# Stores moved to ScalarE's queue, evictions ahead of the first exponential, and a new order of loads and of image 0 in a linear attention layer

## What is computed

```
g = x as (image, h, w, 32 groups, 8); gn = (g - mean) / sqrt(var + 1e-5)      # over h, w and the 8
q, k, v = split(gn @ W_qkv)                                                     # 256 channels each
k = softmax(k over the 4096 tokens)
context = k^T v                                                                 # 256 x 256 for each image
out = x + ((q @ context) @ W_out + b_out)
```

## Time and profile before

| | us |
|---|---|
| median of 3 runs | 1199.64 |
| lowest, highest | 1195.49, 1200.19 |
| profiled execution, its time | 1202.58 |
| its span | 1200.6 |
| TensorE busy in the span | 1166.4 (97%) |
| ScalarE, VectorE, GpSimd busy | 836.3, 931.0, 627.0 |

### The profile page before, as it was taken

How to read it: one execution, slowest core, us unless ns; L and a number is a source line. 1 busy time by engine, 2 the same in 40 slices (tenths; PEclk the granted TensorE clock), 3 DMA queues, 4 the chain that set the end, 5 groups by cost and what they waited for, 6 DMA issues and landing times.

```text
span 1200.6 us, 21468 instructions
## 1 busy us (share of the span) xinstructions
PE 1166.4 (97%) x8206; PEld 1089.3 (91%) x8206; DVE 931.0 (78%) x2008; ACT 836.3 (70%) x1146; POOL 627.0 (52%) x305
## 2 busy tenths in 40 slices
PE   4999999999999999999999999999999999999998
PEld 3889999989899898998989999899999989999996
DVE  6988779787796877878787797878869788796561
ACT  5667768677685776857777676776857768577764
POOL 7655563645656355553655636456463655536530
PEclk9999999999999999999999999999999999999999
DMA  8438666586766758657486665867657586573524
GB/s 318 163 134 315 228 216 236 179 296 214 258 212 202 263 188 280 228 201 250 165 316 228 215 232 179 303 212 261 214 199 271 179 295 227 198 254 119 190 84 162
DMA packets 107078, 266.70 MB, mean 222 GB/s; under 512 B 10208, under 2 KB 10208, under 8 KB 106976
## 3 DMA queue, kind: packets, MB, share of 16 engines
q1 hardware_dynamic: 106976, 265.33, 63.7%
HBM read 198.18 MB, written 67.11 MB: 221 GB/s over the span
## 4 chain that ended last, share of the span: by engine, by line
PE 82%; DMA 6%; DVE 4%; ACT 3%; issue 2%; POOL 1%; SPq 1%; DVEq 0%; ACTq 0%; POOLq 0%
PE ps_k L460 24%; PE ps_e L625 18%; PE ps_e L634 9%; PE ps_e L542 5%; PE ps_e L554 5%; PE ps_e L544 5%; DMA xs<-in_xt_dram 4%; PE ps_g L554 4%; PE ps_g L544 4%; PE ps_g L542 4%; PE ps_g L573 1%; PE ps_g L590 1%; DMA x_raw<-in_xn_dram 1%; DVE bn L922 1%; DVE e_raw L1054 1%
## 5 line engine op out<-in xcount | busy, mean ns | idle before, releaser
L387 POOL TENSOR_TENSOR xt_lo<-xt_raw,xt_hi 128x1024 fp32r<-128x1024 f32 x128 | 307.5, 2404 | 458.8 <-ACT xt_hi L738 194.1
L393 POOL TENSOR_TENSOR x_lo<-x_raw,x_hi 128x1024 fp32r<-128x1024 f32 x128 | 282.4, 2225 | 59.9 <-ACT x_hi L743 50.5
L994 DVE TENSOR_TENSOR mx<-ps_k,mx 128x256 f32<-128x256 f32 x480 | 203.1, 423 | 72.0 <-ACT e_raw L747 50.2
L795 ACT ACTIVATE o_stage<-ps_e,bias 128x512 f32<-128x512 f32 x253 | 168.8, 687 | 105.5 <-PE ps_e L634 101.5
L460 PE MATMUL ps_k<-wk_hi,xt_hi 128*128 128x256 f32 x1024 | 205.9, 283 | 1.4 <-DVE mx L994 1.2
L460 PE MATMUL ps_k<-wk_lo,xt_hi 128*128 128x256 f32 x1024 | 205.0, 282 | 0.0
L747 ACT ACTIVATE e_raw<-ps_k 128x512 f32<-128x512 f32 x256 | 141.2, 595 | 78.1 <-PE ps_k L460 78.1
L755 ACT ACTIVATE e_hi<-e_raw 128x1024 fp32r<-128x1024 f32 x128 | 134.8, 1053 | 67.2 <-DVE e_raw L1054 45.4
L922 DVE BATCH_NORM_STATS2 bn<-xs 128x6 f32<-128x512 f32 x240 | 153.8, 685 | 33.2 <-DMA xs<-in_xt_dram 31.9
L460 PEld LDWEIGHTS ps_k<-wk_hi,xt_hi 128*128 128x128 f32 x1024 | 164.3, 189 | 10.6 <-issue 2.4
L460 PE MATMUL ps_k<-wk_hi,xt_lo 128*128 128x256 f32 x1024 | 157.5, 282 | 0.0
(11 more groups left out here) (147 smaller groups left out, 2027.6 us busy)
## 6 DMA issues: line engine op xcount, KB each, us to landing
xt_raw<-in_xt_dram SPq DMA_DIRECT2D x128, 512.0 KB, 4.6
x_raw<-in_xn_dram SPq DMA_DIRECT2D x128, 512.0 KB, 3.8
out_dram<-o_stage SPq DMA_DIRECT2D x127, 512.0 KB, 4.5
xs<-in_xt_dram SPq DMA_DIRECT2D x240, 256.0 KB, 5.0
w_setup<-in_w_dram SPq DMA_DIRECT2D x2, 256.0 KB, 9.7
out_dram<-o_stage SPq DMA_DIRECT2D x2, 256.0 KB, 2.0
wk<-in_w_dram SPq DMA_DIRECT2D x1, 256.0 KB, 10.0
wq_t<-in_w_dram SPq DMA_DIRECT2D x1, 256.0 KB, 11.0
```

The source lines that it names most:

```text
L387: nc.gpsimd.tensor_tensor(xt_lo[:, s], xt_raw[:, s], xt_hi[:, s].bitcast(F32), ALU.subtract).then_inc(xt_lo_ready, 1)
L393: nc.gpsimd.tensor_tensor(x_lo[:, s], x_raw[:, s], x_hi[:, s, :, 0:C].bitcast(F32), ALU.subtract).then_inc(x_lo_ready, 1)
L795: nc.scalar.activation(o_stage[:, u % O_SLOTS, h, :], src, ACT.Identity, bias=bias[:, h:h + 1]).then_inc(o_ready, 1)
L994: nc.vector.tensor_tensor(mx[:], tile, mx[:], ALU.max).then_inc(max_done, 1)
```

## The change

**ScalarE and the stores.** Each store is taken from SyncE's program and stands in ScalarE's, behind the second eviction of its chunk; ScalarE first waits for `o_ready`, that is, for its own eviction to have written. The last chunk is stored in two halves there. ScalarE's DMAs go on a queue of their own.

**ScalarE's order in a period.** The eviction of emit 4 is put ahead of `exps(n, 0)`. `xt_high(n, 2)` is put behind the gathers' exponentials and `wk_high`.

**SyncE's order.** It has no stores any more. The halves of `xs` go behind other emits (`XS_AHEAD` for `XS_AFTER`), and the last `xt` chunk of a period is loaded in the next one, behind its second `x` load.

**VectorE's order in a period.** The statistics halves are spread otherwise: ten stand ahead of `key_maxes(n, 3)` where eight stood, and one stands between the block maximum and `shift(n, 0)` where four stood.

**Image 0.** Loads of `x` go two steps later, behind `xs` halves 6 to 9; VectorE has two more statistics halves ahead of the first maximum, and none left between the second block maximum and the shifts there; TensorE's gather takes `gather_high(0, 2)` ahead of `gather_low(0, 1)` and `gather_high(0, 3)` ahead of `gather_low(0, 2)`, and the two statistics products later; GpSimd has one `e_low` fewer and `xt_low` of the next image later; ScalarE has the exponentials ahead of the `xt` work.

```diff
-XS_AFTER = {0: (4, 8), 2: (8, 12), 3: (12, 16)}
-FIRST_XT = (8, 11, 15)
-POOL_LOW = 3
+XS_AHEAD = {0: (4, 8), 1: (8, 12), 2: (12, 14), 4: (14, 16)}
+FIRST_XT = (11, 13, 15)
+FIRST_X = (6, 7, 8, 9)
+POOL_LOW = 2
...
             for q in range(S_SLOTS, CB * NCH):
-                if q < 2 * X_SLOTS:
-                    load_x(0, q - X_SLOTS)
                 sp.wait_ge(bn_done, NCH * CB + q - S_SLOTS + 1)
                 load_xs(1, q)
+                if q in FIRST_X:
+                    load_x(0, FIRST_X.index(q))
...
                 for j in range(X_SLOTS, NCH):
                     sp.wait_ge(g_ps, b * NCH + (j - X_SLOTS + 1))
                     load_x(b, j)
+                    if more and b and j == X_SLOTS + 1:
+                        sp.wait_ge(e_ps, b * (CB * NCH))
+                        load_xt(n, 1 - parity, EMIT_ORDER[NCH - 1])
...
-                    if b == B - 1 and u == NCH - 1:
-                        store_last()
-                    elif not late(b, u, CB - 1):
-                        store(b, u)
-                    if more2 and u in XS_AFTER:
-                        for q in range(*XS_AFTER[u]):
+                    if more2 and u in XS_AHEAD:
+                        for q in range(*XS_AHEAD[u]):
                             sp.wait_ge(bn_done, b * (NCH * CB) + 2 * NCH * CB + q - S_SLOTS + 1)
                             load_xs(b + 2, q)
...
+                def first_gather():
+                    gather(0, 0)
+                    gather_high(0, 1)
+                    gather_high(0, 2)
+                    gather_low(0, 1)
+                    spread_max(0, 1)
+                    gather_high(0, 3)
+                    gather_low(0, 2)
+                    gather_low(0, 3)
+                    gather(0, 4)
+                    stats_mean(1)
+                    gather(0, 5)
+                    gather_high(0, 6)
+                    stats_var(1)
+                    gather_low(0, 6)
+                    gather(0, 7)
...
+            def store(b, u):
+                act.wait_ge(o_ready, b * (CB * NCH) + CB * u + CB)
+                nc.scalar.dma_start(out_chunks[bass.ds(b * NCH + EMIT_ORDER[u], 1)].rearrange("a p h n -> (a p) h n"),
+                                    o_stage[:, u % O_SLOTS]).then_inc(stored[u % O_SLOTS], 16)
...
             def emit(b, u):
                 for h in range(CB):
                     if not late(b, u, h):
                         emit_half(b, u, h)
+                        if b == B - 1 and u == NCH - 1:
+                            store_half(b, u, h)
+                        elif h == CB - 1:
+                            store(b, u)
...
+                if b == 0:
+                    exps(0, 3)
+                    x_high(0, 4)
+                    xt_high(1, 1, 0)
+                    scales(0)
+                    for j in range(HALF, NCH):
+                        exp_high(0, j)
+                        if j < NCH - 1:
+                            x_high(0, j + 1)
+                        exp_exact(0, j)
+                    xt_high(1, 1, 1)
...
                 both_out(4)
+                emit(b, 4)
                 if more:
                     exps(n, 0)
-                emit(b, 4)
...
-            for q in range(1, 5):
+            for q in range(1, 7):
                 bn_half(1, q)
             for j in range(HALF):
                 key_maxes(0, j)
-                for q in ((5, 6), (7, 8), (9,), ())[j]:
+                for q in ((7, 8), (9, 10), (11,), ())[j]:
                     bn_half(1, q)
...
                 key_maxes(n, 2)
-                bn_halves(4, 8)
+                bn_halves(4, 10)
                 key_maxes(n, 3)
                 block_max(n, 0)
                 block_diag(n, 0)
-                bn_halves(8, 12)
+                bn_halves(10, 11)
                 shift(n, 0)
```

More of the change, by code:

```diff
@@ L329, in period @@
                     load_x(b, j)
-                if not more:
-                    for u in range(LATE[0][0], NCH):
-                        store(b - 1, u)
+                    if more and b and j == X_SLOTS + 1:
+                        sp.wait_ge(e_ps, b * (CB * NCH))
+                        load_xt(n, 1 - parity, EMIT_ORDER[NCH - 1])
                 if more2:
@@ L341, in period @@
                 for u, j in enumerate(EMIT_ORDER):
-                    if more2 or (more and j not in DOUBLED):
+                    if u < NCH - 1 and (more2 or (more and j not in DOUBLED)):
                         sp.wait_ge(e_ps, b * (CB * NCH) + CB * u + CB)
@@ L680, in period, with gather_steps @@
                 n, np_ = b + 1, 1 - parity
[L681 to L698 removed]
+                def first_gather():
[14 more added lines that the diff above has]
+                    gather(0, 7)
+                def gather_steps():
+                    gather_high(b, 0)
+                    if more:
+                        stats_mean(n)
+                    gather_low(b, 0)
+                    gather_high(b, 1)
+                    spread_max(b, 1)
+                    if more:
+                        stats_var(n)
+                    gather_low(b, 1)
+                    for j in range(2, NCH):
+                        gather(b, j)
+                if b == 0:
+                    first_gather()
+                else:
+                    gather_steps()
                 if more:
@@ L861, in period @@
                     emit_half(b - 1, *LATE[0])
+                    store(b - 1, LATE[0][0])
                 u_high(b, parity)
@@ L865, in period @@
                     emit_half(b - 1, *LATE[2])
+                    store(b - 1, LATE[2][0])
                 else:
@@ L1164, in _ @@
             key_maxes(0, 4)
-            bn_half(1, 11)
+            bn_half(1, 13)
             key_maxes(0, 5)
```

109 lines of the change are left out of this document (49 added, 60 removed).

## The result

The changed kernel takes 1240.15 us in the median of 4 runs (1234.63 to 1244.68) against 1197.82 of the kernel before (4 runs): ratio 1.0353, 95% interval 1.0316 to 1.0391. It is 42 us slower; the prediction was 7 us faster. The profiled execution took 1234.63 us, with a span of 1232.5.

A forecast was written before the change was run, and what follows sets the result against it. TensorE was taken as the bound, with only its idle time and lower clock to win back. Steady images -5.5, image 0 -4.0 + 1.5, stores +1.0 gave -7.0: 1199.64 to 1192.6 us, 8-in-10 range 1188.5 to 1199.5.

The forecast's parts named there:

- Steady images: the eviction wait: Images 2 to 14: TensorE's wait for emit 4's eviction, 4.9 us over the span, is removed in full where it occurs.
- h: ScalarE's hold by one store: about 0.5 us, with up to 1.56 us possible before TensorE waits.
- That count: From emit 4's end to emit 6's first half: TensorE needs 8.54 us, ScalarE 6.98 us plus the store's hold.
- The term of 1.0 us: Stores on ScalarE in the steady images: 1.0 us allowed in all for new small waits of TensorE.
- Rival 4: Stores on a second queue share the engines, so `x` or `xs` loads land later: 1197.6 us, chance 0.05.
- Rival 5: Store issues on ScalarE wait for SyncE's, delaying emit 6 by 1.04 us in 14 images: 1207.2 us, chance 0.08.
- `x_lo` wait: Late gathers: TensorE's wait for GpSimd's low part of `x`, 2.5 us in 5 waits, goes or nearly.
- Rival 1: Steady images: the median run holds only half of the 5.5 us of waits, giving 1195.4 us; chance 0.17.
- Rival 3: Steady images: the stall only moves by one emit, leaving image 0's gain alone: 1198.1 us, chance 0.08.
- The keys: Image 0: two more statistics halves ahead of the first maximum cost 1.5 us, bounds 0 and 2.5.
- The gather's waits: Image 0: five TensorE waits of 3.59 us; with 1.7 us of missing clock, 4.0 us taken back.
- rival 2: Image 0 gives nothing, as VectorE's delay in the keys cancels the gather's gain: 1195.1 us, chance 0.10.

The follow-up runs named there:

- b_stats_new: The kernel before with only the changed kernel's order of the steady statistics halves, all stores on SyncE's queue: 1291.08 us, ratio 1.0767.
- a_both_undone: The changed kernel with the stores back on SyncE and the steady statistics halves in their old places: 1198.63 us, ratio 0.9998.
- b_steady_rest: The kernel before with the changed kernel's steady-image edits except the stores and VectorE's statistics order: 1197.58 us, ratio 0.9994.

## Why the prediction was wrong

**The term that was missing: the statistics ahead of the maxima.** The step that failed is the one under "Steady images: the eviction wait". It counted: "three of the four statistics halves between block maximum and shift are gone", and never charged the place to which two of them went. VectorE does them ahead of `key_maxes(n, 3)`, with `spread_max` behind it, for which TensorE waits. By the prediction's own data a first price was at hand: two halves of 0.65 us and a wait of 1.70 for `xs`, 3.0 us an image, 42 in 14 images. Measured: `u_hi` comes 3.0 us later (28.1 for 25.1), and since TensorE came for it only at 25.9, its step begins 2.2 us later, some 31 us in 14 images; the edit costs 30.5. That the first price gives the same 3.0 is luck: what sets the time is the landing of half 9 at 23.1 us, and in b_stats_new the same two halves make `u_hi` 5.9 us late. For image 0 the prediction did this very sum and put a price on it; for the 14 images that count it did not.

**The size of the slack: the stores on ScalarE.** h was forecast at 0.5 us and measured 0.57. The issue was forecast at 0.39 us and measured 0.38. The failing step is "At 0.5 nothing shows on TensorE by the count above; ... I allow 1.0 us". That count, 8.54 against 6.98 us, ran from emit to emit alone. ScalarE also evicts the keys of the next image in between, and the last of these start a chain (maxima, block diagonal, variance parts) with TensorE at its end. Its slack ended below 0.54 us, not at 1.56. The term of 1.0 us measured 14, of which the hold alone is 5; the rest is mostly the collision of emit 2's store with the `xs` loads, for which the sum had no term.

**Rival 4 was right in kind.** It had a load that lands later since a store shares the engines, priced at the wait for `x_lo` that doubles. It was `xs`, and 5 to 7.6 us. That the rival too stood 5 us above the sum is luck, since its price was that of another load. As the Trainium skill has it ("DMA: Bandwidth & Descriptors", Issuing engines are not separate DMA queues), DMAs of two issuers interleave on the same engines: the landings of the table agree, a store that went from 24.5 to 26.3 us beside loads that went from 25.1 to 25.8.

**Rival 5, the slower one, was wrong.** No issue on ScalarE took over 0.46 us in 127, so none waited 1 us for SyncE's; those that overlapped one of SyncE's took 0.03 us more than the others in the median. The verdict slower, to which only this rival gave a chance, came by other ways. The Trainium skill's lock wait ("Perfetto Trace Analysis", DMA Instruction — HWDGE), a shared generator that one issuer locks while the other waits inside its issue, is not seen here with two issuers, unless as these 0.03 us.

**Right, and worth nothing.** The eviction wait and the `x_lo` wait went as described (to 0.4 and 0.8 us). But the sum took them from one execution, the longest of its kernel; a_both_undone and b_steady_rest, with these edits and without the two dear ones, are at 0.9998 and 0.9994. Rival 1 had named it, and took half of it off; it was all. Rival 3, by which the stall would move to emit 6, was wrong: only 0.4 us of waits for an eviction is left.

**Image 0.** The keys were forecast 1.5 us later, with a bound of 2.5. TensorE's first gather begins at 51.0 us, 3.0 later than before, with waits of 4.5 us in all for the maxima. The gather's waits fell from 3.59 to 2.8 (forecast was that most of them go), and the first window's granted clock rose from 0.98 to 1.00, as forecast. The first combine begins at 81.3 us against 80.8. So image 0 lost 0.5 us in the two profiled executions instead of gaining 2.5: rival 2, with the price of the keys above its bound.

## What to carry over

Work that is moved away from one wait must be charged at the place where it arrives: list who stands behind it there, and when its data lands, since an instruction whose load has not landed costs the landing time and not its duration. A slack is that of the tightest of all chains that run through the engine, not of the one in view; lengthening the engine's work by a dummy of known length, in two sizes, finds it in two runs. Before a wait of a profile is counted as a gain, the profiled execution's own time belongs beside the spread of the runs. And a wait of TensorE can cost more than its length, where the granted clock falls behind it.

## What the hardware showed

A DMA issue by ScalarE costs it 0.38 us, and with the wait for its own eviction to have written 0.57 us from one instruction to the next. Stores of 512 KB in flight beside loads on another queue land 1.8 us later than ahead of them on the same one (26.3 against 24.5 us), and the four loads 0.7 to 0.8 later. The price of a hold was not proportional: 0.54 us cost 5 us, 0.91 us cost 22. Behind waits of TensorE of up to 6.5 us in each of 14 images (b_stats_new) the granted clock fell to 1.2 GHz each time, and the work behind took 1.2 to 2.2 us longer; behind the changed kernel's waits of up to 2.1 us it fell in 2 of 14 images.
